# Loading the expert registers of all slots ahead of the first tile, in a macaron block of two mixture-of-experts layers on one core

## The reference

```python
def ffn_ref(x):                      # the outer layers
    h = rmsnorm(x, ln1_w)
    ...                              # causal attention, 16 heads of 8, added to x
    h = rmsnorm(x, ln2_w)
    probs = softmax(h @ router_w)    # 8 experts
    topv, topi = top_k(probs, 2)     # two experts a token, weights normalised
    gate, up = h @ w_gate[e], h @ w_up[e]          # 128 -> 448
    act = silu(gate) * up * weights
    return x + act @ w_down          # 448 -> 128, summed over experts

x = x + 0.5 * ffn_ref(layernorm(x))
x = x + attn_ref(layernorm(x))
x = x + 0.5 * ffn_ref(layernorm(x))
```

## Time and profile before

| | |
|---|---|
| median of 3 runs | 1879.0 us (1865.26 to 1879.83) |
| profiled execution | 1875.93 us |
| its span, first to last instruction | 1873.9 us |
| mean granted TensorE clock | 0.925 |
| TensorE busy | 1668.0 us, 89% |
| VectorE busy | 1361.2 us, 73% |
| ScalarE busy | 1130.6 us, 60% |
| GpSimd busy | 429.7 us, 23% |

### The profile page before, as it was taken

One profiled execution on the slowest core, in us unless ns is written; L12 is line 12 of the kernel. 1 busy time (PEld: TensorE's weight loads), 2 busy tenths in 40 slices (PEclk: granted clock), 3 DMA queues, 4 the chain that ended last, 5 costly groups with the idle time before them and its releaser, 6 DMA issues. The chain is left out here.

```text
span 1873.9 us, 31569 instructions
## 1 busy us (share of the span) xinstructions
PE 1668.0 (89%) x11226; PEld 768.8 (41%) x11226; DVE 1361.2 (73%) x2852; ACT 1130.6 (60%) x2403; POOL 429.7 (23%) x485
## 2 busy tenths in 40 slices
PE   5899999999858847899999999879999999994985
PEld 3333333333348834233333333423333333323884
DVE  7888998987153348888999984488889998815333
ACT  5355767677735434356767678525577777783554
POOL 6103201111025525030102020230311010211553
PEclk9788999999969977889999999868899999996998
DMA  5400203200011134200202000241011020001113
GB/s 159 111 1 3 52 3 110 62 2 2 8 42 37 39 102 141 52 2 2 53 3 52 3 2 1 72 137 40 2 27 29 2 53 2 2 1 41 37 39 85
DMA packets 49442, 75.45 MB, mean 40 GB/s; under 512 B 9527, under 2 KB 39804, under 8 KB 47736
## 3 DMA queue, kind: packets, MB, share of 16 engines
q1 hardware_dynamic: 43144, 61.94, 12.6%
q0 software_dynamic: 4992, 9.40, 2.0%
q10 hardware_dynamic: 1152, 2.10, 0.3%
HBM read 52.86 MB, written 21.46 MB: 40 GB/s over the span
## 5 line engine op out<-in xcount | busy, mean ns | idle before, releaser
L782 ACT ACTIVATE probs<-ps 128x512 f32<-128x512 f32 (+3 forms) x1920 | 879.0, 543 | 470.0 <-PE ps L915 468.4
L624 DVE TENSOR_REDUCE mpart<-ps 128x1 f32<-128x512 f32 (+3 forms) x1680 | 1015.1, 666 | 115.2 <-PE ps L869 63.7
L869 PE MATMUL ps<-ka,qa 96*128 96x512 bf16 (+3 forms) x1920 | 671.1, 372 | 35.7 <-DMA ka<-ksplit 23.0
L915 PE MATMUL ps<-qa,ka 96*128 96x512 bf16 (+3 forms) x1920 | 616.0, 357 | 0.8
L928 PE MATMUL ps<-probs,vv 128*9 128x512 f32 (+3 forms) x3840 | 441.8, 532 | 8.9 <-ACT probs L782 8.1
L731 POOL TENSOR_SCALAR_AFFINE_SELECT probs<-probs 128x512 f32<-128x512 f32 x192 | 121.8, 634 | 1166.7 <-ACT probs L782 1166.7
L869 PEld LDWEIGHTS ps<-ka,qa 96*128 96x128 bf16 x1920 | 192.2, 101 | 479.4 <-DVE mpart L624 335.7
L915 PEld LDWEIGHTS ps<-qa,ka 96*128 96x128 bf16 x1920 | 183.7, 100 | 186.8 <-ACT probs L782 69.2
L1179 PE MATMUL ps<-hT,probs 128*112 128x128 f32 x1248 | 159.0, 283 | 21.5 <-ACT probs L1209 12.3
L872 PE MATMUL ps<-mask_rows,identb 128*128 128x128 bf16 x768 | 162.3, 236 | 0.0
L1179 PEld LDWEIGHTS ps<-hT,probs 128*112 128x112 f32 x1248 | 147.6, 183 | 29.8 <-ACT probs L1209 15.5
(11 more groups left out here) (179 smaller groups left out, 927.6 us busy)
## 6 DMA issues: line engine op xcount, KB each, us to landing
qa<-qsplit SPq DMA_DIRECT2D x27, 384.0 KB
ka<-ksplit SPq DMA_DIRECT2D x27, 384.0 KB
probs<-rope SPq DMA_DIRECT2D x12, 512.0 KB, 6.6
qa<-qsplit SPq DMA_DIRECT2D x36, 96.0 KB
ka<-ksplit SPq DMA_DIRECT2D x36, 96.0 KB
qsplit<-arena SPq DMA_DIRECT2D x6, 384.0 KB, 3.2
ksplit<-arena SPq DMA_DIRECT2D x6, 384.0 KB, 2.9
tokens<-arena SPq DMA_DIRECT2D x2, 1040.0 KB, 3.9
```

The source lines that it names most:

```text
L624: dve.tensor_reduce(mpart[:, j % MD, h0:h0 + some, qt, kc], ps[:, bank, 0:some * w].rearrange("p (h w) -> p h w", h=some), axis=AX.X, op=A ...
L782: act.activation(probs[:, s % 2, h, 0:n], ps[:, u % SB, 0:n], ACT.Exp, scale=SCALE).then_inc(probs_ready, 1)
L869: ins = pe.matmul(dst, qa[0:KROWS, b, h0 + k, tile * 128:(tile + 1) * 128], ka[0:KROWS, b, h0 + k, kc * CH:kc * CH + n], start=True, stop= ...
L915: pe.matmul(dst, ka[0:KROWS, b, h, kt * 128:(kt + 1) * 128], qa[0:KROWS, b, h, c * CH + q0:(c + 1) * CH], start=True, stop=True).then_inc( ...
```

## The change

In each of the two expert layers, TensorE loads the expert numbers of all 39 slots into 39 registers in a row, right behind its wait for `experts_found`, and only then runs `turn(0)`. The load in the loop is gone; the down products read the register of their slot as before. Nothing is changed on the other engines; below L1166 the line numbers fall by one.

```diff
                     pe.wait_ge(weights_loaded, 48)
                     pe.wait_ge(weights_scaled, 2)
                     pe.wait_ge(experts_found, 1)
+                    experts = [pe.value_load(eti[0:1, u:u + 1], min_val=0, max_val=E - 1) for u in range(NSLOT)]
                     turn(0)
-                    experts = []
                     for i in range(NSLOT + 1):
                         if 1 <= i and i + 1 < NSLOT:
                             turn(i + 1)
                         if i < NSLOT:
-                            experts.append(pe.value_load(eti[0:1, i:i + 1], min_val=0, max_val=E - 1))
                             pe.wait_ge(expert_copied, i + 1)
                             pe.wait_ge(tile_copied, i + 1)
                             if i >= 2:
```

## The result

The changed kernel takes 1925.9 us (median of 4 runs, 1918.15 to 1927.90), the kernel before 1874.8 us in the runs beside it. The ratio is 1.0265, with a 95% interval from 1.0236 to 1.0294: **slower by 50 us**. 1918 us had been forecast, some 40 us over before, with a range of 1896 to 1936. The profiled execution took 1926.64 us, its span 1924.9 us: 51.0 us over the span of before.

A forecast was written before the change was run, and what follows sets the result against it. TensorE, busy 89%, and the first tile's chain of gather, transpose and products were taken as the bound. Loads ahead +41.8 us, loads removed -1.6, sum +40.2 on a median of 1879.0: forecast 1918 us, range 1896 to 1936.

The forecast's parts named there:

- The added stretch: Between last search product and first transpose: 39 loads at 0.65 us delay the transpose 20.9 us a layer, +41.8 us together.
- two lower ends that the prediction gives: Lower ends of the forecast time's range: 1903 us in the sum, 1896 us where the range is stated last.
- Rival 1: Loads ahead of the first tile overlap, 0.3 us each: +7.0 us a layer, 1891 us, within 1%; chance 0.09.
- rival 3: Loads ahead of the first tile all cost 0.9 us: 1938 us; chance 0.07, including what lies between it and the forecast.
- the durations alone: Lower bound for loads ahead of the first tile: 0.47 us each by execution time, +13.7 us a layer, +27 in all.
- What is taken away: In the slot loops, one load fewer per slot, worth nothing where TensorE is fed ahead: gain of -1.6 us.
- rival 2: Slot loops speed up without their loads, up to 51 us back, to 1870 us; chance 0.06 to a draw, 0.02 over 1% faster.
- the loop should begin at the same 0.50 and climb after the same amount of work: At the loop's start: TensorE's clock, already 0.50 in the wait before the first transpose, loses nothing by the change.
- what does wait for the load are four slots: In the loops, four slots show L1179's weight load idle behind the transpose, 1.2 us in all; 0.4 more for such first-slot delays.
- The other engines: At the first tile: ScalarE, VectorE wait for TensorE's delayed work; GpSimd gains no lead, its seven gathers ahead done at 545.9.

The follow-up runs named there:

- e3: Kernel before with 20 of TensorE's 39 loads per layer moved ahead of the first tile, 19 left in the loop: 1900.3 us, ratio 1.0142.
- e4: Changed kernel with another 39 loads ahead in each layer, registers unread: 1971.6 us, ratio 1.0533 to the kernel before.
- e1: Kernel before without 38 of TensorE's 39 loads per layer; every down product takes slot 0's expert, so results are wrong: 1875.6 us, ratio 1.0019.
- e7: Kernel before without the gathers of slots 8 to 38, reusing the first 8 tiles; TensorE's loads stay in the loop: 1840.7 us, ratio 0.9821.
- e8: Changed kernel, all 39 loads ahead, without the gathers of slots 8 to 38: 1877.7 us, ratio 1.0026 to the kernel before.
- e2: Kernel before with its loop loads kept and 39 more, unread, ahead of the first tile in each layer: 1913.7 us, ratio 1.0219.
- e6: Kernel before with ScalarE's load of the next slot's expert number issued ahead of its copy of the turned tile: 1881.3 us, ratio 1.0032.
- e9: Kernel before with the gathers of slots 8 to 38 replaced by SyncE loads of 128 consecutive token rows: 1839.0 us, ratio 0.9824.
- e10: Kernel before with a ring of 20 tiles for 8, so 18 gathers ahead of the first scatter: 1887.6 us, ratio 1.0083.
- e12: Kernel before with a ring of 11 tiles for 8, so 9 gathers ahead: 1869.4 us, ratio 0.9986.
- e5: Kernel before with 16 of 39 loads per layer moved ahead, only where TensorE waits anyway, 23 left in the loop: 1877.3 us, ratio 1.0026.
- e11: Changed kernel with a ring of 20 tiles for 8: 1912.3 us, ratio 1.0219 to the kernel before.

## Why the prediction was right, and its one wrong term

**The added stretch** came as worked out. Loads 0.65 us apart (measured 0.655 and 0.653), the first 0.9 (0.87, from 536.5 to the second load at 537.4), cover of 4.8 and 4.6 us, half clock throughout: +20.9 a layer had been forecast, +20.7 and +20.8 came. So of the 50 us the 41.5 were forecast with their mechanism. That the rest came out small is in part luck: it is the sum of a gain and a larger loss, neither of which the prediction had. Of the two lower ends that the prediction gives, 1903 and 1896, the last line has the second; the measured time lies above both. Rival 1, overlapping loads, is excluded by the step between loads, and rival 3 by the same: only the first load of the first layer cost 0.9. e3 and e4 show that the front goes by the count, each load beyond the cover at its full price. The rule that the Trainium skill gives in "Perfetto Trace Analysis", section "Sequencer-only Instruction (DRAIN, etc)", by which the profile has only the execution of such an instruction, decided the right way: the durations alone, 0.465 us x 39, would have made +27 us of it, and the time between them, which the profile does not show as executing, is 0.19 us of every load.

**What is taken away** was the term that failed. I had put it at -1.6 us, since the load in the loop was nearly free; the two loops together came out 6.7 us longer in the profiles, and the rest by the medians is +8.2 us, with some 5 to either side. In a fed slot it is free, and rival 2, the loop gaining 41 to 51 us, is dead with e1, which has no load in the loop and is not faster. But two things were missed. The first is a gain: without a load between the first products the clock rose earlier. Together with the time of the load that is missing there this is worth 4.3 us in the changed kernel, and it is all of the difference of the loops of e7 and e8. The step that failed there is "the loop should begin at the same 0.50 and climb after the same amount of work". Of fourteen loops with a load in every slot (before, e2, e6, e7, e9, e10, e12) the rise came 9.7 to 9.9 us behind the first transpose in twelve, and 4.2 and 4.3 in the first layers of e2 and e12; of fourteen whose first slots have none (changed kernel, e1, e3, e4, e5, e8, e11) never later than 6.6. What sets it off is open. The second is a loss: the slots behind the first took 11.0 us longer in the changed kernel. The rest of the table is +8.2 us there, +3.6 in e1, +9.7 in e3, +7.8 in e4, +5.1 in e5, all with the loads gone from some or all slots; with them kept, in e2, it is -0.2. Each of these has 3 to 6 us of uncertainty, but five stand on one side. e6, which keeps TensorE's loads and moves only ScalarE's, is 6 us slower too, so by the medians alone another disturbance of the rhythm could do the same. For the missing loads speak, inside one execution, the two halves of e5's first loop: 3.52 us a slot without, 3.10 with. The last loop of before had the faster rhythm and lost 7.9 us, the first had less of it and lost 3.1. e8 against e7 gives the condition: without indirect gathers in the loop nothing is lost behind the first slots. So the step "what does wait for the load are four slots" read single slots rightly and missed that the slots are paced by an interplay with the gathers, in which a slot without its load makes the round longer and not shorter. Slots over 4 us are 10 and 10 in the two loops of the changed kernel, for 11 and 5 before.

One part of the loss can be seen in the windows. In each loop of the changed kernel the clock falls once to half speed for about 3.4 us in a long slot, which it never does in the loops of before, of e2, e4, e7 and e8. Two such falls can cost an estimated 3.4 of the 11.0 us at most:

```profile
646.60:650.00 3.40, 3.40 (x18) 3.40 (x18) 1.77 (x7) 1.80 (x3) 0.82 (x1) 0.50 0.11 27
```

What this interplay looks like, in the timeline of the changed kernel: the transpose at 640.87 takes 0.27 us, GpSimd issues a gather (L1114) at 642.06, and ScalarE starts its copy at 643.93, 2.8 us after the transpose's end. The next transpose waits for this copy until 644.36, and the one behind it comes only 5.70 us later:

```profile
640.87 0.27 PE L1160 MATMUL ps<-identf,arena 128*128 128x128 f32 x1
642.06 0.98 POOL L1114 DMA_INDIRECT arena<-tokens,from_row  x1 [0.30 <-issue]
643.93 0.28 ACT L1201 ACTIVATE hT<-ps 128x128 f32<-128x128 f32 x1 [3.33 <-remote]
644.36 0.30 PE L1160 MATMUL ps<-identf,arena 128*128 128x128 f32 x1 [0.57 <-ACT hT L1201]
```

In e8 the transpose of 642.64 ends at 642.92 and the copy starts at 642.96; the next transpose comes at 645.40, and so on in each slot:

```profile
642.96 0.28 ACT L1201 ACTIVATE hT<-ps 128x128 f32<-128x128 f32 x1 [0.58 <-PE ps L1160]
```

The waits of ScalarE's copy in the first loop of the changed kernel (total us, times, longest; the longest of 31.9 us is the front) are in part put down to "remote", which means that no release in the record fits:

```profile
ACT hT L1201 <- PE ps L1160: 45.0, 12, 31.9
ACT hT L1201 <- remote: 31.2, 15, 3.3
```

In e8 there is no such row, all 39 are released by the transpose.

By which way a gather holds TensorE's signals up, and why the slots with a load in them suffer less, was not settled: e9 leaves GpSimd's indirect issue as the difference, e10 shows the stall when the gathers come in a row, e11 that TensorE's sequencer falls behind as well and not only the arrival of what it signals, and no run changes the order of waits in the loop. Nor does e1 against the changed kernel settle whether a late start adds to the loss (3.6 for 8.2 us), or whether the falls of the clock in e1, the changed kernel and e3 come of the missing loads: e6, with a load in every slot, has two of them, while e4, with none in any slot, and e5, with none in its first 16, have not one.

**The other engines** behaved as the prediction had it: half clock in the gap, no lead for GpSimd, no wait for the gather at the first transpose. The loops came as long as before to 5 us in the first layer (+1.0) and just not in the last (+5.7).

## What to carry to other kernels

A register load in TensorE's own sequencer costs its step from start to start, here 0.65 us, and what hides it is the work queued on the array; 39 cheap loads gathered in front of the first tile are 25 us of a cold start, while each in its slot hides under the 2 us of matmuls of a fed slot. Before moving such work, measure the wait that is to cover it (here 4.8 us, room for 7 loads). And where slots alternate between two lengths although no engine is full, look for a second queue in their rhythm, before crediting or blaming the few hundred nanoseconds between two of their instructions. The starts of successive slots inside one loop show such a rhythm where the medians of the whole program hardly do.

## What the runs showed of the hardware

Beside indirect gathers issued by GpSimd, the other engines went on late with what TensorE had finished: by 2.8 us in the slot shown above, by over 13 us (552.63 to 566.02, e10) while GpSimd issued them back to back. In e11 the step of TensorE's own register loads grew from 0.656 to 1.48 us towards the end of such a row, though nothing stood in their way that the profile shows. Taking 31 gathers out of each loop brought 33.5 us in all (1874.2 - 1840.7), and loading the same number of bytes by SyncE's queue in their place cost nothing (1839.0 us for 1840.7). Scatters issued by GpSimd, one a slot in all these kernels, left the slots at 2.75 us where the gathers were gone.

TensorE's granted clock rose from 0.50 to 1.00, 1.2 to 2.4 GHz, between 4.2 and 9.9 us after the first transpose, with nearly the same products in the first slots; two layers of one kernel, e2, stand at 4.2 and 9.8. Where a load stood between the first products it was mostly the long one. In long slots of some loops it fell back to half speed for 3.4 us, and in e10, where TensorE stood still for 2.67 and 8.24 us, for 13.7 us.
